# Attention scores of a cross-attention layer: unsplit float32 queries and keys, sixteen 32x32 products side by side in place of three rounds of four 32x128 products

## The reference, cut to what matters

```
x:   1 x 4096 x 512        context: 1 x 3202 x 512       16 heads of 32

q = layernorm(x) @ Wq + bq     k = context @ Wk + bk     v = context @ Wv + bv
scores = einsum('blhe,bshe->bhls', q, k)                 # 4096 x 3202 for each head
A = softmax(scores / sqrt(32), axis=-1)
x = x + einsum('bhls,bshd->blhd', A, v) @ Wo + bo
x = x + top-2-of-8 experts(layernorm(x))                 # router and expert matrices 512 x 512
```

## Time and profile before

| | |
|---|---|
| median of 3 runs | 2379.47 us (2377.31 to 2384.11) |
| the profiled execution | 2381.51 us |
| its span, first to last instruction | 2379.7 us |
| mean granted TensorE clock | 0.981 |
| busy: TensorE 96%, VectorE 85%, ScalarE 78%, GpSimd 21% of the span | |

### The profile page before, as it was taken

How to read it: one execution, slowest core, us unless ns; L and a number is a source line. 1 busy time by engine, 2 the same in 40 slices (tenths; PEclk the granted TensorE clock), 3 DMA queues, 4 the chain that set the end, 5 groups by cost and what they waited for, 6 DMA issues and landing times. The chain is left out here.

```text
span 2379.7 us, 49163 instructions
## 1 busy us (share of the span) xinstructions
PE 2275.9 (96%) x19632; PEld 1097.8 (46%) x19632; DVE 2018.2 (85%) x1866; ACT 1855.5 (78%) x2155; POOL 508.8 (21%) x631
## 2 busy tenths in 40 slices
PE   8999699999999999999999999999999999789898
PEld 7878533333333333333333333333333357578786
DVE  4358489999999999999999999999999988867565
ACT  3223299999999999999999999999999956534332
POOL 2213211311111111111111111111111113146664
PEclk9999899999999999999999999999999999889999
DMA  7436564345464455557444434644544467634463
GB/s 267 168 135 213 179 168 108 90 110 114 112 178 108 110 128 134 132 133 199 108 112 112 117 90 128 155 114 108 117 97 101 101 175 266 205 106 141 147 205 120
DMA packets 140924, 333.70 MB, mean 140 GB/s; under 512 B 28918, under 2 KB 61654, under 8 KB 123548
## 3 DMA queue, kind: packets, MB, share of 16 engines
q0 software_dynamic: 43008, 193.75, 33.8%
q1 hardware_dynamic: 95356, 129.20, 16.6%
q10 hardware_dynamic: 2336, 7.60, 0.9%
HBM read 131.16 MB, written 82.78 MB: 90 GB/s over the span
## 5 line engine op out<-in xcount | busy, mean ns | idle before, releaser
L1133 ACT ACTIVATE probs<-psum 128x1536 f32<-128x1536 f32 x800 | 1164.7, 1456 | 0.0
L1300 PE MATMUL psum<-probs,v_st 128*32 128x512 f32 x6400 | 853.2, 605 | 0.2 <-ACT probs L1133 0.2
L1251 PE MATMUL psum<-q_st,k_st 32*128 32x512 f32 x9600 | 779.1, 425 | 43.2 <-ACT probs L1130 27.4
L1251 PEld LDWEIGHTS psum<-q_st,k_st 32*128 32x128 f32 x9600 | 402.2, 183 | 745.5 <-ACT probs L1130 431.0
L1207 DVE TENSOR_TENSOR even_sums<-even_sums,probs 128x2048 f32<-128x2048 f32 x288 | 658.6, 2287 | 75.6 <-ACT probs L1133 74.6
L1207 DVE TENSOR_TENSOR odd_sums<-odd_sums,probs 128x2048 f32<-128x2048 f32 x256 | 588.4, 2299 | 3.1 <-ACT probs L1133 3.1
L1130 ACT ACTIVATE probs<-psum 128x512 f32<-128x512 f32 x800 | 481.0, 601 | 40.1 <-PE psum L1251 32.4
L1300 PEld LDWEIGHTS psum<-probs,v_st 128*32 128x32 f32 x6400 | 126.1, 108 | 289.0 <-issue 278.8
L2087 PE MATMUL psum<-we_hi,wo 128*128 x624 | 219.1, 412 | 7.6 <-ACT wo L1926 4.4
L948 POOL DMA_DIRECT2D pile<-probs x96 | 85.2, 888 | 495.4 <-DMA pile<-probs 308.2
L2087 PEld LDWEIGHTS psum<-we_hi,wo 128*128 128x128 f32 x624 | 119.7, 192 | 34.4 <-issue 8.7
(11 more groups left out here) (229 smaller groups left out, 2262.8 us busy)
## 6 DMA issues: line engine op xcount, KB each, us to landing
pile<-probs POOLq DMA_DIRECT2D x128, 1024.0 KB, 7.5
token_rows<-rows SPq DMA_DIRECT2D x8, 1028.0 KB, 6.7
xn<-in_x SPq DMA_DIRECT2D x16, 512.0 KB, 6.5
qh_scratch<-o_hi SPq DMA_DIRECT2D x8, 1024.0 KB, 4.5
ql_scratch<-o_lo SPq DMA_DIRECT2D x8, 1024.0 KB, 7.5
q_st<-qh_scratch SPq DMA_DIRECT2D x32, 256.0 KB, 4.4
q_st<-ql_scratch SPq DMA_DIRECT2D x32, 256.0 KB, 5.1
token_rows<-in_x SPq DMA_DIRECT2D x8, 1024.0 KB, 7.6
```

The source lines that it names most:

```text
L1133: act.activation(probs[:, p, 1:HG, :], psum[:, bank(t, 1):bank(t, 1) + HG - 1, :], ACT.Exp, bias=-WIDEST, scale=SCALE).then_inc(exp_done, 1)
L1251: return nc.tensor.matmul(psum[:, bank(t, h), :], k_st[rows, part, t * P:(t + 1) * P], q_st[it % 2][rows, of, :], start=start, stop=stop)
L1300: mm = nc.tensor.matmul(psum[h * DH:(h + 1) * DH, bank, :], lhs(h), rhs(h), start=start, stop=stop)
```

## The change

Keys and queries are no longer split. ScalarE writes one float32 result `o_sb`, `k_low` and `q_low` go, one store and one load take the place of two, and the waits on the low part become waits on ScalarE's result (`k_out`, `q_out`). In attention, a head's 128 keys are cut in four pieces of 32. For each of the four pieces and each of the four heads there is one float32 matmul of 32 rows x 32 columns x 512 queries, with no second or third term; the piece picks the strip of the array's columns (and the PSUM partitions), the head the strip of its rows. `rest_scores` becomes one float32 matmul. The shifted branch is changed in the same way.

```diff
-TERMS = ((0, 0), (0, 1), (1, 0))
...
-        o_hi = [sb(f"o_hi{b}", [P, NG, CH], F32R) for b in range(2)]
-        o_lo = [sb(f"o_lo{b}", [P, NG, CH], F32R) for b in range(2)]
+        o_sb = [sb(f"o_sb{b}", [P, NG, CH], F32) for b in range(2)]
...
                 def store_q(c, b):
-                    sp.wait_ge(q_hi, (c + 1) * NG)
-                    sp.wait_ge(q_lo, (c + 1) * NG)
-                    sp.dma_start(qh_d[:, :, ds(c * CH, CH)], o_hi[b][:].bitcast(F32)).then_inc(q_stored[b], 16)
-                    sp.dma_start(ql_d[:, :, ds(c * CH, CH)], o_lo[b][:].bitcast(F32)).then_inc(q_stored[b], 16)
+                    sp.wait_ge(q_out, (c + 1) * NG)
+                    sp.dma_start(q_d[:, :, ds(c * CH, CH)], o_sb[b][:]).then_inc(q_stored[b], 16)
...
-                def k_low(c, b, w):
-                    for j in range(NG):
-
-                        dve.wait_ge(k_hi, c * NG + (j + 1))
-                        dve.scalar_tensor_tensor(out=o_lo[b][:, j, 0:w], in0=psum[:, j, 0:w], scalar=bk_col[:, j:j + 1],
-                                                 in1=o_hi[b][:, j, 0:w].bitcast(F32), op0=ALU.add, op1=ALU.subtract).then_inc(k_lo, 1)
...
-                    pe.wait_ge(k_lo, c * NG)
+                    pe.wait_ge(k_out, c * NG)
...
-        k_st = sb("k_st", [P, 2, S], F32R)
+        k_st = sb("k_st", [P, S], F32)
...
-            for part, src in enumerate((kh_d, kl_d)):
-                sp.dma_start(k_st[:, part:part + 1, first:first + n].bitcast(F32), src[:, ds(j, 1), first:first + n]).then_inc(count, 16)
+            sp.dma_start(k_st[:, first:first + n], k_d[:, ds(j, 1), first:first + n].rearrange("p o s -> p (o s)")).then_inc(count, 16)
...
-                def products(it, t, h, term, start, stop):
-
-                    part, of = TERMS[term]
-                    rows = slice(h * DH, (h + 1) * DH)
-                    return nc.tensor.matmul(psum[:, bank(t, h), :], k_st[rows, part, t * P:(t + 1) * P], q_st[it % 2][rows, of, :], start=start, stop=stop)
+                def queries_of(it, part):
+
+                    return q_st[it % 2][:, part, :].bitcast(F32)
...
-                    for term in range(len(TERMS)):
-                        last = term == len(TERMS) - 1 and not shifted
+                    for o in range(0, P, DH):
                         for h in range(HG):
-                            mm = products(it, t, h, term, term == 0, last)
+                            rows = slice(h * DH, (h + 1) * DH)
+                            mm = nc.tensor.matmul(psum[o:o + DH, bank(t, h), :], k_st[rows, t * P + o:t * P + o + DH], queries_of(it, 0)[rows, :], start=True, stop=not shifted)
...
-                    for term, (part, of) in enumerate(TERMS):
-                        mm = nc.tensor.matmul(psum[0:REST_ROWS, REST_BANK, :], rest_k[:, j, part, 0:REST_ROWS], q_st[b][:, of, :],
-                                              start=term == 0, stop=term == len(TERMS) - 1 and not shifted)
+                    mm = nc.tensor.matmul(psum[0:REST_ROWS, REST_BANK, :], rest_k[:, it // NC, 0:REST_ROWS], queries_of(it, 0), start=True, stop=not shifted)
```

More of the change, by code:

```diff
@@ L195, in projections @@
         v_mm = sem("v_mm")
-        k_hi = sem("k_hi")
-        k_lo = sem("k_lo")
+        k_out = sem("k_out")
         v_out = sem("v_out")
@@ L272, in store_kv @@
                 def store_kv(c, b, w):
[L274 to L277, removed]
+                    sp.wait_ge(k_out, (c + 1) * NG)
+                    sp.dma_start(k_d[:, :, ds(c * CH, w)], o_sb[b][:, :, 0:w]).then_inc(k_stored[b], 16)
                     if w == CH:
@@ L539, in x_low @@
                                           ALU.subtract).then_inc(x_lo, 1)
[L541 to L544, removed]
-                                                 in1=o_hi[b][:, j, :].bitcast(F32), op0=ALU.add, op1=ALU.subtract).then_inc(q_lo, 1)
                 def q_search(c):
@@ L550, in _ @@
                 ln(0, 0, 0)
-                k_low(NSC - 1, 0, last_w)
                 v_chunk(NSC - 1, 0, pairs, last_w)
@@ L556, in q_chunk @@
                 def q_chunk(c, b, i):
-                    q_low(c, b, range(half))
                     if not (isinstance(c, int) and c == 0):
@@ L563, in q_chunk @@
                         ln(c + 2, b, i + 1)
-                    q_low(c, b, range(half, NG))
                 q_chunks(dve, q_chunk)
@@ L620, in v_products @@
                         if t == min(1, w // P - 1):
-                            pe.wait_ge(k_lo, c * NG + 1)
+                            pe.wait_ge(k_out, c * NG + 1)
                             sum_squares(c, K_SUM_BANK, w, k_squared, k_summed)
@@ L678, in _ @@
                 pe.wait_ge(ident_ready, 2)
-                pe.wait_ge(k_lo, NSC * NG)
+                pe.wait_ge(k_out, NSC * NG)
                 pe.wait_ge(k_searched, NSC)
@@ L719, in load_queries @@
 def load_queries(sp, g, b, it, count):
-    for part, src in enumerate((g["qh_d"], g["ql_d"])):
-        sp.dma_start(g["q_st"][b][:, part, :].bitcast(F32), src.rearrange("p j l -> p (j l)")[:, ds(it * CH, CH)]).then_inc(count, 16)
+    sp.dma_start(g["q_st"][b][:, 0, :].bitcast(F32), g["q_d"].rearrange("p j l -> p (j l)")[:, ds(it * CH, CH)]).then_inc(count, 16)
 def load_shift(sp, g, b, it, count):
@@ L803, in attention @@
     S, SP_, NG, NC, NT, LAST, SCALE, D, L = (g[n] for n in "S SP_ NG NC NT LAST SCALE D L".split())
-    kh_d, kl_d, v_d, qh_d, ql_d, shift_d = (g[n] for n in "kh_d kl_d v_d qh_d ql_d shift_d".split())
+    k_d, v_d, shift_d = (g[n] for n in "k_d v_d shift_d".split())
     NIT = NG * NC
@@ L1043, in _ @@
                 load_k(sp, 0, 0, piece_end(0), first_k_in)
[L1044 to L1045 removed]
+                sp.dma_start(rest_k_raw[:], k_d[:, :, S - LAST:S]).then_inc(rest_k_in, 16)
                 sp.dma_start(v_st[:, 0:pieces[0][1], :], v_d[:, 0:pieces[0][1], 0:P]).then_inc(first_v_in, 16)
                 with sp.If(sp.value_load(unbounded[0:1, 0:1], min_val=0, max_val=1) == 1):
[L1048 to L1049 removed]
+                    sp.wait_ge(q_in[0], 16)
+                    sp.wait_ge(first_k_in, 16)
                     with sp.Fori(0, NG) as j:
@@ L1267, in scores @@
                         pe.wait_ge(first_done, it * NT + t)
-                    for term in range(len(TERMS)):
-                        last = term == len(TERMS) - 1 and not shifted
+                    for o in range(0, P, DH):
                         for h in range(HG):
-                            mm = products(it, t, h, term, term == 0, last)
+                            rows = slice(h * DH, (h + 1) * DH)
+                            mm = nc.tensor.matmul(psum[o:o + DH, bank(t, h), :], k_st[rows, t * P + o:t * P + o + DH], queries_of(it, 0)[rows, :], start=True, stop=not shifted)
                     if shifted:
-                        for h in range(HG):
-                            row = slice(h * DH, h * DH + 1)
-                            mm = nc.tensor.matmul(psum[:, bank(t, h), :], shift_ones[row, :], q_st[it % 2][row, SHIFT_PART, :], start=False, stop=True)
+                        for o in range(0, P, DH):
+                            for h in range(HG):
+                                row = slice(h * DH, h * DH + 1)
+                                mm = nc.tensor.matmul(psum[o:o + DH, bank(t, h), :], shift_ones[row, 0:DH], queries_of(it, SHIFT_PART)[row, :], start=False, stop=True)
                     mm.then_inc(s_ready, 1)
                 def rest_scores(it, shifted):
-                    b, j = it % 2, it // NC
                     pe.wait_ge(exp_done, it * STEPS + REST_TILE - 1)
@@ L1367, in _ @@
                                             w = min(CH, S - b * CH)
-                                            for term, (part, of) in enumerate(TERMS):
-                                                mm = pe.matmul(psum[:, b, 0:w], q_st[0][rows, of, t * P:(t + 1) * P],
-                                                               k_st[rows, part, b * CH:b * CH + w], start=term == 0, stop=term == len(TERMS) - 1)
+                                            mm = pe.matmul(psum[:, b, 0:w], queries_of(0, 0)[rows, t * P:(t + 1) * P],
+                                                           k_st[rows, b * CH:b * CH + w], start=True, stop=True)
                                         mm.then_inc(ma_mm, 1)
-                    pe.wait_ge(ma_q_in, (NIT * 2 + 3) * 16)
+                    pe.wait_ge(ma_q_in, (NIT + 2) * 16)
                     for it in range(NIT):
```

105 lines of the change are left out of this document (48 added, 57 removed).

## The result

The changed kernel takes **2532.1 us** (median of 4 runs, 2530.2 to 2533.9), against 2379.1 us for the kernel before on the same chip (4 runs): 1.064 times the time, with a 95% interval of 1.062 to 1.066. The forecast was 2514 us, with a range of 2450 to 2660.

The account below looks back on a forecast made before the run. TensorE was taken to bound the kernel. From the profiled 2381.5 us, 144 for longer scores and rest, -4 for waits and -4.5 for projections gave 2517, stated as 2514 us since unprofiled runs are 2 us shorter; range 2450 to 2660.

Parts of the forecast that it names:

- TensorE sets the pace: In attention before the change, TensorE's groups follow without idle time, 1.893 us a tile; ScalarE has 0.08 us to spare.
- the first rival: Scores and weigh no longer need a change of the array's shape: 1.84 us a tile, kernel 2335 us; chance 6%.
- The price of sixteen pieces, weigh's 1.00 + 12 x 0.007 = 1.08: Attention scores cost weigh's time plus twelve more starts: 1.08 us against 0.90, 0.18 us more a tile.
- sixteen under way within 0.1 us: Sign in a steady tile's scores: sixteen matmuls under way within 0.1 us of the first.
- 24 of 25 tiles pay: In each attention step all tiles but the one behind `fetch` pay 0.18 us, 4.3 us a step.
- Rest, +0.18: The rest's once-a-step float32 product takes some 0.93 us against 0.75, 0.18 us more.
- Waits that go, -4: In a few attention steps ScalarE's waits for a free `probs` buffer shrink, and loads move half: -4 us.
- TensorE can't be fed: Rival: instructions for 80 records a tile arrive too slowly; at 0.030 us each, 2.40 us a tile, some 2780 us; 13%.
- Projections, -4.5: At the projections' end, attention no longer starts behind the low part's store: -4.5 us.
- ScalarE idle 0.26 us a tile: Sign in a steady attention tile: ScalarE stands idle 0.26 us a tile.

Follow-up runs that it names:

- eight pieces with full piles: The changed kernel with scores as eight float32 products of 64 keys, summing DMAs left whole; 2480.2 us, 1.042 times the kernel before.
- small piles: The changed kernel with summing DMAs moving only head 0's quarter once the first step is done; 2514.1 us, 1.056 times the kernel before.

## Why the prediction was right, step by step

**TensorE sets the pace**: right. The pace after is 2.083 us against the 2.07 forecast, weigh to scores stayed at 0.99 to 1.00 us, so the first rival is out. The reading behind it, that a change of shape costs 0.12 us each way in which nothing starts, was the wrong name for the right size: these 0.12 us are the group's first load, 0.10 to 0.18 us by its number of columns, and its starts; no run leaves more than 0.01 us beside them.

**The price of sixteen pieces, weigh's 1.00 + 12 x 0.007 = 1.08**: right in mechanism and size, 1.09 measured. The reading that four strips and sixteen tiles behave alike held: two passes side by side, and starts as the only further cost. The twelve further starts take 0.10 us in place of 0.08, and the sign "sixteen under way within 0.1 us" came at 0.12. By the Trainium skill, "TensorE: Matmul & The Clock Gate", Part 3, starts and ends of matmuls keep a strict order; if a product's two passes stood next to each other in the stream, as the prediction put it, that would have given 17 passes, 7.3 us. The trace has 1.09 us for sixteen pieces, as it has 1.00 for four; in which order the passes stand in the stream no row shows, so either that condition or the rule doesn't hold here. The 4 ns between starts that the same part gives is not what the float32 products show (7 ns).

**24 of 25 tiles pay**: right. Tile by tile (medians over the steps), the tile behind `fetch` takes 2.62 us as before, set by ScalarE; all others take 0.19 more.

**Rest, +0.18**: 0.15 measured (the tile with the rest takes 4.32 us in place of 3.98, of which 0.19 are its scores). Together 4.66 us a step against 4.5, 5 us in 32 steps.

**Waits that go, -4**: right by itself. In the kernel before, ScalarE's first exponential waits 7.4 us for piled buffers:

```profile
L1130 ACT ACTIVATE probs<-psum 128x512 f32<-128x512 f32 x800 | 481.0, 601 | 40.1 <-PE psum L1251 32.4 <-DMA pile<-probs 7.4
```

After has none of these waits, and eight pieces with full piles are only 0.7 us over 31 of their undisturbed steps. But at this term the forecast missed something: it looked for irregular waits that vanish and put new ones at nothing. The mean step is 0.56 us above the undisturbed one, more than the 0.20 before: 31 x 5.01 = 155 us, where the forecast's 31 x 4.5 - 4 makes 135. The new waits are those of the rival "TensorE can't be fed", 13% in the forecast, which came true in small. The forecast had priced it as a rate (a tile of 80 records at 0.03 us each), and that isn't what happened: fetching keeps up in every undisturbed tile, and fails in 14, for some 1.1 us each, when a packet of instructions stands behind a summing DMA.

**Projections, -4.5**: right in size. The end of the projections and the start of attention, as in the earlier trace rows:

```profile
273.77 0.53 SPq L299 DMA_DIRECT2D q_scratch<-o_sb  x1
...
279.22 0.35 SPq L859 DMA_DIRECT2D k_st<-k_scratch  x1
...
SPq L320 <- DMA q_scratch<-o_sb: 3.6, 1, 3.6
```

```profile
286.74 1.17 PE L1238 MATMUL psum<-q_st,k_st 32*32 32x512 f32 x16 [8.89 <-issue]
```

The store issued at 273.77 is the last one, and scores start at 286.74 where 287.5 was forecast. The wait of the SP queue for a store, which the forecast read as the price of the low part, is still there, 3.6 us in place of 4.0. The 4.8 us by which attention's first load is issued earlier (279.22 against 284.01) are 2.25 for the earlier issue of the last store, some 2.2 for one shorter issue of a load in place of two, and 0.4 of the wait.

**ScalarE idle 0.26 us a tile**: 0.15 in the record (1003.54 - 1003.39). The forecast took ScalarE's pace while catching up, 1.81 us, as its busy time. There the next exponential (809.95) starts 0.12 us before the record of the last ends; apart from each other the two of a tile take 1003.39 - 1001.46 = 1.93 us. No time hung on it.

**Error of the sum.** The forecast made 2517 of the profiled execution's own time; it came to 2532, 15 us more. In the 31 steps it is 19.9 us more: 5 in the undisturbed steps and some 15 in the new gaps, net of the old waits. Outside them it is 4.8 us less: the forecast has 4.5 for the 32nd step and -4.5 for the projections, measured are -5.8 and +1.0. Of that, 2.5 us lie behind attention, in a stage that the change doesn't touch, so a part of how near the forecast came is luck. That small piles give 2514.1, the forecast's number, shows no more than that the steady part was right.

## What to carry to other kernels

Full float32 costs two passes of 0.43 us for 512 columns, and a tile of scores on TensorE's path then costs 1.04 to 1.09 us, against 0.90 for three rounds of split operands: splitting was the cheaper way here, and how finely the array is cut moves only the second digit. Price such a group as first load + starts + passes; 64 keys a piece are best here, since the first load is shorter than with 128 and the starts are fewer than with 32. Count instructions beside passes: doubling their number cost the steady tile no more than the starts, but brought 16 us in which TensorE had no instructions, behind large DMAs on another queue. When a trace shows gaps for "issue" inside a group that waits for no semaphore, look in the DMA view for the packets of instructions and for the transfer ahead of them.

## What the runs showed of the hardware

- Sixteen 32x32 float32 products run at the same time, each with its second pass 0.45 us behind the first (1002.66 - 1002.21), whichever of heads or keys is in the inner loop.
- One start costs 0.007 us for a float32 product, which has four records, for the first fourteen of sixteen in a group of 64 records, and 0.015 to 0.017 us for the last two; 0.017 us in the second half of a group of 128.
- Between groups of another shape the first load stands in the open: 0.101 us for 32 float32 columns, 0.127 for 64, 0.181 for 128. First load, starts and 0.87 us for two passes of 512 columns make up the group's time in all four forms measured.
- A packet of 16 KB of TensorE's instructions, some 250 records, can stand behind a summing DMA that keeps the DMA engines at 81% for 7 us, and matmuls go on 1.0 to 1.6 us after it has landed. With that DMA a quarter as large, the 14 stops vanish.
